# Attention b in row-and-column quadrants with a new order of work on VectorE, and three statistics groups moved to ScalarE

## The reference

```python
x = x + attn_a(layernorm(x))   # 16 heads of width 8, sparse mask
x = x + ffn(layernorm(x))      # 8 experts, one for each token by argmax of an affinity
x = x + attn_b(layernorm(x))   # 16 heads of width 64, causal softmax
x = x + ffn(layernorm(x))      # the same FFN again
```

## Time and the profile before

| What | us |
|---|---|
| median of the timed runs | 528.8 |
| the profiled execution | 524.73 |
| its span, first to last instruction | 522.9 |
| attention a, about | 84 |
| first FFN's preparation | 38 |
| first FFN | 54 |
| attention b with the second preparation inside | 261 and a start of 12 |
| end of the second preparation | 15 |
| second FFN | 59 |

### The profile page before, as it was taken

One profiled execution on the slowest core, in us unless ns is written; L12 is line 12 of the kernel. 1 busy time (PEld: TensorE's weight loads), 2 busy tenths in 40 slices (PEclk: granted clock), 3 DMA queues, 4 the chain that ended last, 5 costly groups with the idle time before them and its releaser, 6 DMA issues.

```text
span 522.9 us, 11650 instructions
## 1 busy us (share of the span) xinstructions
PE 433.8 (83%) x3882; PEld 340.7 (65%) x3882; DVE 370.5 (71%) x1466; ACT 253.6 (49%) x867; POOL 239.0 (46%) x250
## 2 busy tenths in 40 slices
PE   2857896634999289999999999999999998439993
PEld 1324555523999246787777778777776787339992
DVE  6699998961666358857779687796879776456661
ACT  1641000512444037758757678576774857115450
POOL 6100988471455224544435345463445546314453
PEclk9987999555999689999999999999999999859997
DMA  8999930034673200000000000000000000136640
GB/s 310 359 389 422 419 158 1 22 106 118 213 207 116 85 2 2 1 1 3 1 1 4 1 1 13 11 21 3 1 11 12 22 1 22 42 101 203 195 140 6
DMA packets 22234, 48.98 MB, mean 94 GB/s; under 512 B 3328, under 2 KB 13574, under 8 KB 19744
## 3 DMA queue, kind: packets, MB, share of 16 engines
q1 hardware_dynamic: 18880, 40.86, 22.3%
q0 software_dynamic: 3296, 7.39, 4.5%
HBM read 24.99 MB, written 24.15 MB: 94 GB/s over the span
## 4 chain that ended last, share of the span: by engine, by line
PE 62%; DVE 17%; issue 6%; ACT 5%; POOL 5%; DMA 3%; POOLq 0%; SPq 0%; DVEq 0%; ACTq 0%
PE ps L868 9%; PE ps L881 8%; PE ps L924 8%; PE ps L999 6%; PE ps L1012 6%; PE ps L966 5%; PE ps L941 4%; PE ps L931 4%; ACT vT L657 3%; PE ps L758 3%; POOL vT L520 2%; PE ps L776 2%; PE ps L716 2%; POOL sorted_in L490 2%; DVE prod L1110 2%
## 5 line engine op out<-in xcount | busy, mean ns | idle before, releaser
L520 POOL TENSOR_TENSOR vT<-vT,prec 128x256 f32<-128x256 f32 (+1 forms) x128 | 103.1, 826 | 129.5 <-DVE prec L1446 128.7
L657 ACT ACTIVATE vT<-vT,nmax 128x128 f32<-128x128 f32 (+1 forms) x256 | 113.4, 448 | 14.3 <-DVE nmax L1436 14.1
L1436 DVE CUSTOM_DVE_ANT_0 vT<-ps,cst 128x128 f32<-128x128 f32 (+1 forms) x256 | 77.5, 350 | 5.4 <-PE ps L966 5.3
L665 ACT COPY prod<-ps 128x384 f32<-128x384 f32 x96 | 42.9, 482 | 60.6 <-PE ps L999 60.6
L924 PE MATMUL ps<-xnT,wb 128*128 128x256 f32 x256 | 68.0, 389 | 1.4 <-DVE qk L1417 0.9
L999 PEld LDWEIGHTS ps<-cst,vT 128*128 128x128 f32 x384 | 42.7, 141 | 30.7 <-POOL vT L520 15.3
L999 PE MATMUL ps<-cst,vT 128*128 128x128 f32 x384 | 54.5, 278 | 4.1 <-POOL vT L520 3.1
L1417 DVE COPY qk<-ps 128x512 f32<-128x512 f32 x64 | 43.4, 678 | 13.6 <-PE ps L924 13.5
L881 PE MATMUL ps<-w2s,pv 128*128 (+1 forms) x368 | 49.3, 277 | 0.8 <-issue 0.8
L924 PEld LDWEIGHTS ps<-xnT,wb 128*128 128x128 f32 x256 | 44.8, 195 | 7.6 <-DVE qk L1417 2.4
L657 ACT ACTIVATION_READ_ACCUMULATOR vT<-vT,nmax 128x1 f32 x256 | 49.0, 191 | 0.0
(11 more groups left out here) (150 smaller groups left out, 794.6 us busy)
## 6 DMA issues: line engine op xcount, KB each, us to landing
sorted_in<-zero SPq DMA_DIRECT2D x1, 16512.0 KB, 64.8
pv<-in_w SPq DMA_DIRECT2D x30, 259.0 KB, 4.0
pv<-sorted_in SPq DMA_DIRECT2D x46, 129.0 KB, 2.8
wps<-in_w SPq DMA_DIRECT2D x1, 2072.0 KB, 9.4
w2s<-in_w SPq DMA_DIRECT2D x1, 2048.0 KB, 14.1
wb<-in_w_b SPq DMA_DIRECT2D x1, 1536.0 KB, 22.9
xres<-in_x SPq DMA_DIRECT2D x4, 256.0 KB, 3.9
xres<-in_bo_a POOLq DMA_DIRECT2D x2, 512.0 KB, 13.8
```

The lines of the kernel that those rows point to most:

```text
L520: last = nc.gpsimd.tensor_tensor(px, px, view(prec, m_at(n, x) + t * 2, [[1, 2], [0, (t + 1) * P]]), ALU.mult)
L657: last = nc.scalar.activation(px, px, ACT.Exp, bias=nmax[:, m:m + 1], scale=-1.0, accum_out=psum[:, m:m + 1])
L1436: ins = nc.vector.tensor_tensor_reduce(out=pb[:, o:o + w], in0=wide[:, c:c + w], in1=cst[:, mask:mask + w], scale=-1.0, scalar=-MASKED * 2 ...
```

## The change

Attention b:

- The values of a step become two parts of 8 matmuls each, in 64 x 64 quadrants, into two banks instead of one. Part 0 stands where `values_b` stood; part 1 follows in the next step, between the scores of pair 0 and those of pair 1. Keys of the second tile are kept in the order 3, 2 (`PLACES`), so that masked key blocks are skipped for half a tile; query block 2's scores become two matmuls instead of one.
- Scores of the two pairs are signalled apart. Q and K of the two pairs go to two other banks, the transposes too.
- DVE: `copy_z` moves between the maxima of the two heads of pair 0, `invert(n, 1)` behind all four maxima of pair 0, and the preparation (`norm`, `choose`, `count`, `place`, and before step 24 `means` and `spread`) from the end of the step to a place between `invert(n1, 0)` and `copy_p(n)`. `norm` comes one step later than before.
- ACT: `exp_b(n1, 0, [0])` moves ahead of the first two copies, `exp_b(n1, 0, [1])` ahead of `copy_v` and the third copy.

First FFN's preparation: the statistics of groups 0 to 2 are made on ACT by sums with accumulators while attention a still runs (`moments`), a copy of token numbers moves from DVE to ACT, attention a's last round sums four slots on PE instead of a second addition on POOL (`add_up`), and `choose` and `norm` change order. `spread` has two independent instructions where it had four dependent ones (both FFNs).

```diff
 # ACT, step
+if ok(n1): exp_b(n1, 0, [0])
 if ok(n): copy_p(n, 0, 1); copy_p(n, 0, 0)
-if ok(n1): exp_b(n1, 0, [0])
+if ok(n1): exp_b(n1, 0, [1])
 ... copy_v(n, (j + 2) % STEPS)
 if ok(n): copy_p(n, 1, 1)
-if ok(n1): exp_b(n1, 0, [1])
 if ok(n1): exp_b(n1, 1)
 # PE, step
 scores_b(n1, 0)
+values_b(at(b, j - 1), 1)
 scores_b(n1, 1)
 ...
-values_b(n)
+values_b(n, 0)
 # PE, values_b
+if part == 0:
+    pe.wait_ge(b_pa, 3 * nth(n) + 3)
+    pe.wait_ge(b_pd, nth(n) + 1)
+    pe.wait_ge(b_v, least(nth(n) + 3, NB * STEPS))
+    if ok(at(n[0], n[1] + 2)):
+        pe.wait_ge(b_qk, 2 * nth(n) + 5)
+    need(pe, b_z, nth(n))
+else:
+    pe.wait_ge(b_ph, nth(n) + 1)
+for kt in range(T):
+    for r in range(2):
+        x, k, rows = r ^ part, QUERIES[kt][r], slice(r * HALF, (r + 1) * HALF)
 # DVE, step, the new order
+scored(n1, 0); max_b(n1, 0, 0, 0 and 1)
+copy_z(at(b, j - 1))
+max_b(n1, 0, 1, 0 and 1)
+invert(n, 1)
+scored(n1, 1); max_b(n1, 1, ...) x4
+copy_qk(n2, 0)
+invert(n1, 0)
+norm, choose, count, place, means and spread where due; statistics_b
+copy_p(n)
+copy_qk(n2, 1)
+copy_xT, residual_b, norm_b where due
 # ACT, after attention a's exponentials
+for g in range(NG - 1):
+    moments(g)
 # DVE, first preparation
-for g in range(2):
-    means(0, g)
-    spread(0, g)
+norm(0, 0)
 residual_a(NU - 1)
```

More of the change, by code:

```diff
@@ L1015, in values_b @@
-                last.then_inc(b_pv, 1)
+                            last = nc.tensor.matmul((bank[1], bank[2])[x][hh * DHB:(hh + 1) * DHB, k * HALF:L],
+                                                    vb[rows, v:v + DHB], pT[rows, c:c + L - k * HALF],
+                                                    start=kt == 0 and part == 0, stop=kt == T - 1 and part == 1,
+                                                    skip_group_check=True)
+                last.then_inc((b_ph, b_pv)[part], 1)
@@ L1361, in ffn @@
                 finish(NSLOT - 1)
-            nc.vector.tensor_copy(view(pack, 2 * D + 1, [[ROW, NT]]), cst[:, C_TOKEN:C_TOKEN + NT])
-            dve.wait_ge(a_x, NU - 1)
-            for g in range(2):
-                means(0, g)
-                spread(0, g)
-            residual_a(NU - 1)
-            norm(0, 0)
-            means(0, 2)
-            spread(0, 2)
-            norm(0, 1)
-            choose(0, 0)
-            count(0, 0)
+            norm(0, 0)
+            residual_a(NU - 1)
             dve.wait_ge(a_x, NU)
@@ L1377, in _ @@
             spread(0, 3)
+            choose(0, 0)
+            count(0, 0)
+            norm(0, 1)
             place(0, 0)
@@ L1507, in step @@
                     spread(1, g)
+            def step(b, j):
+                n, n1, n2 = (b, j), at(b, j + 1), at(b, j + 2)
+                bv = b + j // 2
+                if ok(n1):
+                    scored(n1, 0)
+                    for t in range(T):
+                        max_b(n1, 0, 0, t)
+                if ok(at(b, j - 1)):
+                    copy_z(at(b, j - 1))
+                if ok(n1):
+                    for t in range(T):
+                        max_b(n1, 0, 1, t)
+                if ok(n):
+                    invert(n, 1)
+                if ok(n1):
+                    scored(n1, 1)
+                    for hh in range(2):
+                        for t in range(T):
+                            max_b(n1, 1, hh, t)
+                if ok(n2):
+                    copy_qk(n2, 0)
+                if ok(n1):
+                    invert(n1, 0)
+                g = due("powers", at(b, j - 1))
+                if g is not None:
+                    norm(1, g)
+                g = due("affinity", n)
+                if g is not None:
+                    choose(1, g)
+                if nth(n) != LAST:
+                    g = due("count", n)
+                    if g is not None:
+                        count(1, g)
+                    g = due("rank", n)
+                    if g is not None:
+                        place(1, g)
+                    if nth(n) < AMID:
+                        prepared(n)
+                if n in ((-1, 3), (0, 0), (0, 1)):
+                    statistics_b(nth(n) + 2)
+                if ok(n):
+                    copy_p(n)
+                if ok(n2):
+                    copy_qk(n2, 1)
+                if j == 1 and some(b + 1):
+                    copy_xT(b + 1)
+                if j == 0 and some(b - 1):
+                    residual_b(b - 1)
+                if j == 0 and some(b) and some(b + 1):
+                    norm_b(b + 1)
+                if nth(n) == LAST:
+                    count(1, due("count", n))
+                    place(1, due("rank", n))
+                elif nth(n) >= AMID:
+                    prepared(n)
             statistics_b(0)
```

243 lines of the change are left out of this document (122 added, 121 removed).

## The result

| | median, us | runs |
|---|---|---|
| before | 528.61 | 528.21 to 530.34 |
| changed | 543.4 | 542.57 to 544.48 |
| changed / before | 1.027 | 95% interval 1.0241 to 1.0299 |

The change made the kernel 2.7% slower, 14.8 us, where 545.0 was forecast. The profiled execution has a span of 542.2 us, 19.3 more than the 522.9 of before.

A forecast was written before the change was run, and what follows sets the result against it. PE set the pace before; afterwards a closed loop through ACT would. Steps 3 to 29 +16.8, first preparation -1.8, attention b's start +1.3 make +16.3 on 528.8: 545 us; 8-in-10 range 524 to 552.

The forecast's parts named there:

- The closed loop of a plain step: Attention b's steps without preparation: scores, ACT's chain and values part 0 form a loop without slack; 6.92 us, 0.17 more.
- three chains: Plain step of attention b: ACT's chain sets 6.92 us, with POOL's division at 6.2 and DVE's `copy_p` at 6.1 just below.
- PE alone: Plain step: PE's own need 6.50 us, 0.20 saved on the values' columns and 0.05 on the mode change.
- the drain: Tiling-mode changes on PE: one of three goes away, so PE's need falls a little more than columns say; counted for a rival.
- The preparation in its new place: DVE, before `copy_p` in attention b: a piece X makes the step 6.75 + X, so `means` steps 8.05, `norm` with projection 13.2.
- POOL's blocking: Attention b: POOL's division of n1 holds DVE's preparation instructions, so `norm` ends at 8.35 and its step takes 9.55, with projection 13.2.
- the rival without it: Attention b: slower, but POOL doesn't block the preparation; +8 - 0.5, total 531.5 to 538 us; chance 0.20.
- Steps 3 to 29: Attention b's steps, plain ones and those with preparation together: +16.8 us.
- The first preparation: First FFN's preparation: statistics on ACT let the first indirect DMA start near 98.6 instead of 100.4; -1.8 us (-3 to -0.5).
- The rest: Outside steps 3 to 29: first preparation -1.8, start of attention b +1.3, end 0.
- The start of attention b: Statistics of three sequences now stand between the first reciprocal and POOL's power: +1.3 us (0 to +3).
- The end: Second preparation: two instructions go (-0.4), `norm` of two tiles stands ahead of a `copy_p` (+0.5); put at 0.

The follow-up runs named there:

- experiments 2 to 4: Changed kernel with: pair 1's reciprocal earlier, 543.43 us; V and third copies ahead of head 1's exponentials, preparation, `copy_p`, `invert(n1, 0)` in that order, 516.44; both, 512.99.
- experiment 4: Changed kernel with early `invert(n, 1)`, ACT's V and third copies before head 1's exponentials, and DVE order preparation, `copy_p(n)`, `invert(n1, 0)`: 512.99 us, 0.9778 of before.
- experiment 8: Experiment 4's kernel with both parts of the values together at the end of the step: 536.19 us, 1.0214 of the kernel before.
- Experiment 1: Changed kernel with DVE's preparation and the start's statistics ahead of `invert(n1, 0)` instead of behind it: 519.92 us, 0.9901 of the kernel before.
- the repeat: The changed kernel timed and traced once more, nothing altered: 537.4 us, 1.0227 of the kernel before.
- experiment 2: Changed kernel with DVE's `invert(n, 1)` right behind `copy_z`, ahead of the maxima of pair 0's second head: 543.43 us, 1.034 of the kernel before.
- experiment 9: Changed kernel with PE's output projection ahead of the transposes of the preparation's normalized tiles: 542.54 us, 1.0295 of the kernel before.
- experiments 9 and 10: Output projection moved ahead of the normalized tiles' transposes: in the changed kernel, 542.54 us (1.0295 of before), and in experiment 4's kernel, 517.33 us (0.9811).

## Why the prediction was right

**The closed loop of a plain step** was the right picture, with an error of 0.15 us. ACT started 2.67 after the scores (2.70 forecast), its chain took 3.45 (3.44), PE followed 0.06 later (0.16), and a part cost 0.59 (0.62): 6.77, not 6.92. That three chains lie close together was right too, and experiments 2 to 4 are the proof: take one away and nothing happens, take both and the step is 6.46, where PE alone was forecast to need 6.50. The third, `copy_p` on DVE, ended at 257.24 in the plain step, 0.25 before part 0, and no run takes it away alone. I had ACT's chain 0.1 above POOL's, and the trace has it 0.04 above. Of the 0.25 us that PE alone was to save, 0.20 came from the columns and 0.05 from the change of mode; no run shows that 0.05. Scores and values together took 2.35 us in experiment 4 where 2.70 had stood, so they saved more than both, and the rest of the step gave 0.06 back.

The Trainium skill (TensorEngine Tiling (Array Packing), Key Properties) says that a change of tiling mode drains the array. No run here prices the drain. Experiment 4, with one change of mode fewer than before, saved 0.15 us more on these parts than the columns say. But experiment 8 changes mode as often as experiment 4 and takes 2.67 us for the same matmuls, where 2.70 had stood: neither the columns' 0.20 nor the drain shows there. What the rule is worth stays open; the order of the parts counts for more.

**The preparation in its new place** was the main term, and its mechanism was right. The place costs what stands between the reciprocal and `copy_p`; the base is 6.60 and not 6.75, for `copy_p` starts 5.40 into a plain step (5.5 forecast) and the next scores follow 1.2 to 1.37 after its start. Most entries with a preparation are therefore 0.13 to 0.35 too high (step 25 was 0.18 too low, and so was the input's step 5, by 0.17). `place` was off by 0.7: I took 0.79 for a cast from the earlier trace rows, and it took 0.38 here. POOL's blocking was there and near the forecast size for `norm` (2.54 for the piece; 1.41 was its unblocked length), and the rival without it stood lower than the steps came out. Over steps 3 to 29 the truth lies between the two, though: the forecast had +16.8, the rival about +8, and without the clock drop it was +11.5. Experiment 1 confirms the place in two ways, by the shorter instructions and by the 16 us that come back.

The Trainium skill (SBUF — State Buffer, Who interferes with whom) has a DVE instruction with two SBUF inputs, or a tensor-scalar in a mode that uses two ports, blocked by a GpSimd instruction which reads SBUF. The trace agrees for the instruction with two inputs, L1311: 0.48 against 0.16 us. The tensor-scalar L1314 was held too (1.91 against 1.12); whether it ran in such a mode no run here shows.

**Steps 3 to 29** came to +13.4 where the sum had +16.8. It would have been some +11.5 by the terms that I had, for one of the steps 12 and 20 holds a clock drop in the changed kernel, in its repeat and in experiment 2 (1.84, 1.51 and 1.62 us), after 1.93 to 2.26 us of idle time; in experiment 9 both hold it, after 2.44. That term was missing altogether: I priced idle time of PE at its own length.

**The first preparation.** The forecast was -1.8 (-3 to -0.5), with the first DMA at 98.6. It came at 99.2 in the changed kernel; alone it came at 98.15. The whole term was -3.7 us in the timed runs, of which 1.1 is what the shorter `spread` gave in attention b, the part that was missing; the 2.6 that are left lie within the range. In the changed kernel's profiled execution DVE's idle stretches turned the gain round: the first FFN began at 126.80, before the change at 124.83, in the repeat at 123.35. Whether the changed kernel's timed executions had these stretches the times don't show.

**The rest.** The start of attention b (steps -1 to 2) cost +1.05, +1.3 forecast, and +1.97 in the repeat with its clock drop in step 0; experiment 1 shows that the place of the statistics was the cause, since it took back 1.70. The end, from the last `scores_b` to the second FFN, was put at 0; it was 34.22 against 31.74 us, and 31.99 in the repeat, so 0.25 of it repeats. The other 2.2 lie between the last values and the transposes of the last tiles (9.74 us, 7.43 in the repeat), where the granted clock fell to 0.50 at 15.7 us after the last scores, in the repeat at 18.0; why isn't shown. The profiled executions add up: +2.4 to the first scores, +1.05, +13.4, +2.5, +0.1 for the second FFN, 19.3 in all. Errors of both signs met in the sum: the body was 3.4 too high even with a clock drop in it that nobody had forecast, and the end and the idle stretches were missing. That the total came within 1.6 us of 545.0 is therefore in part luck; by the repeat's ratio of 1.0227 the loss is 12.0 us where +16.3 was forecast.

## What to carry to other kernels

When several engines hand work to each other in a closed loop, lay out each engine's order on one clock and look for the chains that end together: freeing one alone gives nothing (0.04 and -0.07 us a step here), freeing both gave 0.31, and took the kernel from -1.0% (experiment 1) to -2.2%. Work that fills gaps belongs in front of an engine's wait and not behind it; one reciprocal's distance was worth some 14 to 16 us of 540. And an engine's own saving (here 0.3 us of PE for each step) is only worth what the next chain lets through, which the waits of one step show and the busy share (83% and 80%) doesn't.

## What the runs showed of the hardware

- Idle times of PE of 1.80 to 2.27 us, between stretches of full work, were followed by a granted clock of 0.50 (1.2 GHz) for some 3.4 us now and then: in the changed kernel, its repeat and experiment 2 in one of the steps 12, 20 and 26 each, every time one with a projection. After 2.44 us it came in both steps of experiment 9, after 1.96 in its step 26 not. After 1.68 us or less it came in none of steps 3 to 29, but two waits of 1.60 us that follow each other in step 0 had it in two of five traces. The fall stood anywhere from 0.3 us before the end of the idle time to 1.4 behind it. It cost 1.5 to 1.8 us each time in a step with a projection, nearly as much again as the wait.
- A DVE instruction that POOL's division held ended within 0.1 us of the end of POOL's instruction (296.18 and 296.16, 297.24 and 297.16), however short it is alone (0.16 and 0.35 us).
- Sixteen quadrant matmuls of the values take 0.54 us between score matmuls in quadrants and 0.59 ahead of them, but thirty-two in a row take 1.46, and not twice that. What makes the difference wasn't tried.
- DVE stood still for 1.2 to 5.4 us at a time in the first preparation, with nothing of the program as releaser, in the changed kernel and in experiments 9 and 10. The page counts this as another core or an unknown queue, 2% of the last chain. Its cause is open.
